# Attention steps of a cross-attention and expert kernel: a new order on three engines, and one 512 KB DMA that turns the two tiles of a head

## The reference

```python
q = jnp.einsum('bnd,de->bne', ln, Wq)                 # ln: normalised x
kv_in = jnp.concatenate([xn, ln], axis=1)             # 512 keys: context and x
kv = jnp.einsum('bnd,de->bne', kv_in, Wkv)
k, v = jnp.split(kv, 2, axis=-1)
q, k, v = (split_heads(q), split_heads(k), split_heads(v))
sim = jnp.einsum('bhid,bhjd->bhij', q * scale, k)
attn = jax.nn.softmax(jnp.where(full_mask[:, None, None, :], sim, max_neg), axis=-1)
out = jnp.einsum('bhij,bhjd->bhid', attn, v)
out = jnp.einsum('bne,ed->bnd', out.transpose(0, 2, 1, 3).reshape(b, m, INNER), Wout)
return layer_norm(out, g_o, b_o)
```

## Time and profile before

| | |
|---|---|
| median of 3 runs | 455.98 us (454.72 to 457.31) |
| the profiled execution | 455.38 us, its span 453.4 us |
| mean granted clock of TensorE, share of full | 0.945 |
| busy: PE, DVE, ACT, POOL | 371.8, 293.6, 263.7, 271.4 us |
| SP's DMA queue (q1), share of 16 engines over the span | 50.7% |
| transposes of tiles | 128, of 256 KB |

### The profile page before, as it was taken

How to read it: one execution, slowest core, us unless ns; L and a number is a source line. 1 busy time by engine, 2 the same in 40 slices (tenths; PEclk the granted TensorE clock), 3 DMA queues, 4 the chain that set the end, 5 groups by cost and what they waited for, 6 DMA issues and landing times. The chain is left out here.

```text
span 453.4 us, 7499 instructions
## 1 busy us (share of the span) xinstructions
PE 371.8 (82%) x2225; PEld 268.7 (59%) x2225; DVE 293.6 (65%) x732; ACT 263.7 (58%) x507; POOL 271.4 (60%) x346
## 2 busy tenths in 40 slices
PE   3669787887878888787889989886249999999996
PEld 2547565664656556465666657554137677777774
DVE  2888774747566574756556465660867777778885
ACT  3767866564645546464655646471058666666681
POOL 3231228677676767768676776872421677777681
PEclk9999998999999999999998989895559999999999
DMA  8200137967977979888999889799000000000001
GB/s 236 54 1 1 23 69 121 182 121 139 184 138 134 170 138 137 169 140 178 132 142 185 121 138 176 135 145 210 0 0 1 2 0 0 0 0 0 1 0 46
DMA packets 154913, 42.76 MB, mean 94 GB/s; under 512 B 144768, under 2 KB 154496, under 8 KB 154880
## 3 DMA queue, kind: packets, MB, share of 16 engines
q1 hardware_dynamic: 154448, 40.78, 50.7%
q10 hardware_dynamic: 432, 1.57, 1.1%
HBM read 8.26 MB, written 0.52 MB: 19 GB/s over the span
## 5 line engine op out<-in xcount | busy, mean ns | idle before, releaser
L394 POOL TENSOR_TENSOR p<-prob,p 128x512 f16<-128x512 f32 x128 | 147.4, 1163 | 90.5 <-ACT p L557 88.7
L549 ACT ACTIVATE prob<-sc,p_bias 128x512 f32<-128x512 f32 x128 | 91.0, 711 | 104.6 <-DVE p_bias L1155 104.5
L1146 DVE CUSTOM_DVE_ANT_0 sc<-ps,mask_add 128x512 f32<-128x512 f32 x128 | 83.0, 682 | 6.6 <-PE ps L706 4.9
L1180 DVE TENSOR_TENSOR q_lo<-ps,q_hi 128x512 fp32r<-128x512 f32 x32 | 22.1, 691 | 88.8 <-ACT q_hi L562 88.8
L704 PE MATMUL ps<-kv_hi,q_hi 128*128 128x512 f32 x128 | 53.5, 418 | 23.4 <-DVE neg_max L1146 23.4
L802 PE MATMUL ps<-pT,v 128*64 128x256 f16 x768 | 53.9, 296 | 4.4 <-DMA pT<-p 4.4
L1338 DVE TENSOR_TENSOR h<-h,ps 128x1024 f32<-128x1024 f32 (+1 forms) x32 | 39.1, 1221 | 18.9 <-PE ps L928 17.7
L802 PEld LDWEIGHTS ps<-pT,v 128*64 128x64 f16 x768 | 46.8, 120 | 6.2 <-issue 4.9
L706 PE MATMUL ps<-kv_hi,q_lo 128*128 128x512 f32 x128 | 50.2, 392 | 0.0
L705 PE MATMUL ps<-kv_lo,q_hi 128*128 128x512 f32 x128 | 50.1, 391 | 0.0
L704 PEld LDWEIGHTS ps<-kv_hi,q_hi 128*128 128x128 f32 x128 | 24.0, 187 | 40.0 <-DVE neg_max L1146 35.2
(11 more groups left out here) (193 smaller groups left out, 746.8 us busy)
## 6 DMA issues: line engine op xcount, KB each, us to landing
pT<-p SPq DMA_TRANSPOSE x128, 3.2
wup_s<-in_L_ffn_W_up SPq DMA_DIRECT2D x8, 256.0 KB, 3.4
wdn_s<-in_L_ffn_W_down SPq DMA_DIRECT2D x8, 256.0 KB, 3.7
wkv_s<-in_L_xattn_Wkv ACTq DMA_DIRECT2D x2, 512.0 KB, 7.1
x_in<-in_x SPq DMA_DIRECT2D x2, 256.0 KB, 8.1
wq_s<-in_L_xattn_Wq ACTq DMA_DIRECT2D x1, 512.0 KB, 7.6
tok<-in_ctx SPq DMA_DIRECT2D x4, 128.0 KB, 8.1
wo_s<-in_L_xattn_Wout SPq DMA_DIRECT2D x1, 512.0 KB, 5.4
```

What stands on the lines that cost most here:

```text
L394: pool.tensor_tensor(p16[:, t, 1, :], prob[:, t, :], p16[:, t, 0, :], ALU.subtract).then_inc(s_plo, 1)
L549: act.activation(prob[:, t, :], sc[:, t, :], ACT.Exp, bias=p_bias[:, t:t + 1], scale=-1.0, accum_out=p_sum[:, i % 2, t:t + 1]).then_inc(s_ ...
L1146: return dve.tensor_tensor_reduce(sc[:, t, :], ps[:, SCORE_BANK + (i * TILES + t) % SCORE_BANKS, :], mask_add[:, i % B, :], -SCALE, -LEAST ...
```

## The change

Four things change, all in the attention steps.

1. **One DMA for a head.** `turn_head` takes both tiles of a head in one transpose of 128 x 2048 values (512 KB). It waits for the low half of the head's second tile. `s_turned` has two semaphores, one for each head, and whoever waited for a tile's turn waits for the head's. `pT` is laid out with the tile outside the block of keys, so that the transpose writes one contiguous run of 16 blocks, and `attend` reads two runs of 128 queries per matmul.
2. **ACT**: exp 0, exp 1, high 0, high 1, query high half, exp 2, exp 3. The quarter of the queries is the one that PE computed in the step before.
3. **DVE**: the output of step i-3 is scaled at the head of the step; `shift_range(i, 2)` comes ahead of `invert(i - 1)`; the query's low half is that of the quarter that ACT now makes in this step.
4. **PE**: `project` behind `attend`. And `neg_max` and `p_bias` have a free element between two used ones.

```diff
@@ -83,7 +83,7 @@
             ("pick16", [P, E], F16), ("ones", [P, P], F32), ("range_v", [P, 8], F32),
-            ("neg_max", [P, TILES], F32), ("p_bias", [P, TILES], F32), ("p_sum", [P, 2, TILES], F32),
+            ("neg_max", [P, TILES, 2], F32), ("p_bias", [P, TILES, 2], F32), ("p_sum", [P, 2, TILES], F32),
             ("p_rinv", [P, 2, TILES], F32),
@@ -96,7 +96,7 @@
             ("p16", [P, TILES, 2, KEYS], F16),
-            ("pT", [P, 2, 2, 2 * KT, QT, P], F16), ("rinv_sb", [P, S], F32), ("ao", [P, S], F32),
+            ("pT", [P, 2, 2, QT, 2 * KT, P], F16), ("rinv_sb", [P, S], F32), ("ao", [P, S], F32),
         ])
@@ -226,7 +226,7 @@
         s_squares, s_range = sem("s_squares"), sem("s_range")
-        s_turned = [sem(f"s_turned{t}") for t in range(TILES)]
+        s_turned = [sem(f"s_turned{head}") for head in range(2)]
@@ -309,17 +309,18 @@
-            def turn_p(i, t):
-
-                sp.wait_ge(s_plo, i * TILES + t + 1)
-                if t == 0 and i >= 2:
+            def turn_head(i, head):
+
+                sp.wait_ge(s_plo, i * TILES + (head + 1) * QT)
+                if head == 0 and i >= 2:
                     sp.wait_ge(s_av, i - 1)
-                sp.dma_start_transpose(pT[:, i % 2, t // QT, :, t % QT, :],
-                                       p16[:, t, :, :].rearrange("p a k -> p (a k)")).then_inc(s_turned[t], 16)
+                sp.dma_start_transpose(pT[:, i % 2, head, :, :, :].rearrange("p q k c -> p (q k) c"),
+                                       p16[:, head * QT:(head + 1) * QT, :, :].rearrange("p t a k -> p (t a k)"))\
+                    .then_inc(s_turned[head], 16)
             for i in range(STEPS):
-                for t in range(TILES):
-                    turn_p(i, t)
+                for head in range(2):
+                    turn_head(i, head)
                 if i % B == 2:
@@ -382,7 +383,7 @@
                 if i:
-                    pool.wait_ge(s_turned[t], 16 * i)
+                    pool.wait_ge(s_turned[t // QT], 16 * i)
                 pool.tensor_copy(p16[:, t, 0, :], prob[:, t, :]).then_inc(s_phi_pool, 1)
@@ -546,14 +547,14 @@
                     act.wait_ge(s_rinv, i - 1)
-                act.activation(prob[:, t, :], sc[:, t, :], ACT.Exp, bias=p_bias[:, t:t + 1],
+                act.activation(prob[:, t, :], sc[:, t, :], ACT.Exp, bias=p_bias[:, t, 0:1],
                                scale=-1.0, accum_out=p_sum[:, i % 2, t:t + 1]).then_inc(s_exp, 1)
...
                 if i:
-                    act.wait_ge(s_turned[t], 16 * i)
+                    act.wait_ge(s_turned[t // QT], 16 * i)
                 act.activation(p16[:, t, 0, :], prob[:, t, :], ACT.Copy).then_inc(s_phi_act, 1)
@@ -596,11 +597,11 @@
                 split_high(i, 0)
+                split_high(i, 1)
+                if 2 <= i <= STEPS - B + 1:
+                    q_high(i + 2, (i - 2) % B)
                 exp(i, 2)
-                split_high(i, 1)
                 exp(i, 3)
-                if i <= STEPS - B:
-                    q_high(i + 3, (i - 1) % B)
@@ -791,17 +792,17 @@
                 pair, b = i // B, i % B
-                for t in range(TILES):
-                    pe.wait_ge(s_turned[t], 16 * (i + 1))
+                for head in range(2):
+                    pe.wait_ge(s_turned[head], 16 * (i + 1))
                 if i:
...
                         cut = slice(head * DH, (head + 1) * DH)
-                        mm = pe.matmul(ps[cut, AV_BANK, 0:S],
+                        mm = pe.matmul(ps[cut, AV_BANK, 0:S].rearrange("p (q c) -> p q c", q=QT),
                                        v16[:, b * KT + j, v, pair * P + head * DH:pair * P + (head + 1) * DH],
-                                       pT[:, i % 2, head, p * KT + j, :, :].rearrange("p q c -> p (q c)"),
+                                       pT[:, i % 2, head, :, p * KT + j, :],
                                        start=(n == 0), stop=(n == len(terms) - 1), skip_group_check=True)
@@ -853,11 +854,11 @@
                         score_step(i, t)
-                if i >= 3:
-                    project(i - 3)
                 if i >= 2:
...
                     attend(i - 2)
+                if i >= 3:
+                    project(i - 3)
                 if i <= STEPS - B:
@@ -1145,14 +1146,14 @@
                                                 mask_add[:, i % B, :], -SCALE, -LEAST, ALU.add, ALU.min,
-                                                neg_max[:, t:t + 1]).then_inc(s_masked, 1)
+                                                neg_max[:, t, 0:1]).then_inc(s_masked, 1)
...
                     dve.wait_ge(s_exp, (i - 1) * TILES + t + 2)
-                dve.tensor_scalar(p_bias[:, t:t + 2], neg_max[:, t:t + 2], LN_RANGE16, None, ALU.add)\
+                dve.tensor_scalar(p_bias[:, t:t + 2, 0], neg_max[:, t:t + 2, 0], LN_RANGE16, None, ALU.add)\
                    .then_inc(s_bias, 1)
@@ -1249,17 +1250,17 @@
             for i in range(1, STEPS):
+                if i >= 3:
+                    normalise_out(i - 3)
                 mask_scores(i, 0)
                 mask_scores(i, 1)
-                if i >= 3:
-                    normalise_out(i - 3)
                 shift_range(i, 0)
...
                 mask_scores(i, 3)
+                shift_range(i, 2)
                 invert(i - 1)
-                shift_range(i, 2)
-                if i <= STEPS - B:
-                    q_low(i + 3, (i - 1) % B)
+                if 2 <= i <= STEPS - B + 1:
+                    q_low(i + 2, (i - 2) % B)
             normalise_out(STEPS - 3)
...
             normalise_out(STEPS - 2)
```

## The result

The changed kernel takes **467.84 us** (median of 4 runs, 467.01 to 469.08) beside 456.47 for the kernel before (4 runs, 454.72 to 457.31): a ratio of 1.0272, 95% interval 1.0240 to 1.0303, so 11.4 us slower by the medians, 12.4 by the ratio, where 4.8 were forecast. The profiled execution has a span of 466.5 us, 13.1 more than before.

A forecast was written before the change was run, and what follows sets the result against it. A POOL and `p_bias` loop of 7.92 us was taken to bound the step; the 7.90 us landing loop eats the order's gain. 455.38 + 1.8 (end) + 3 (halts) = 460.2 us, range 439 to 470.

The forecast's parts named there:

- What bounds the kernel now: Attention steps: a loop of waits through POOL and `p_bias`, 7.92 us, with one through DVE and ACT close by, 7.4.
- The order: New order on ACT, DVE and PE: by itself brings the step to about 7.1 us, 22 us over 28 steps.
- the free element: Gap in `p_bias` on DVE: nothing taken in the sum; if `p_bias` meets POOL's high halves, up to 17 us lost.
- the fast rival: Long transpose lands within 3.72 us, loop 7.25: 439.7 us, up to 457 if `p_bias` meets POOL; chance 0.19.
- the rival by which the order gains nothing: Order doesn't gain even without the DMA, as the query's wait binds PE; time 460 us, no separate chance given.
- X: Time from issue to landing of a 512 KB transpose: 4.37 us, paced by how fast the issue hands out pieces.
- the second head's loop: Landing, POOL's four instructions, issue, landing: 3.53 + X = 7.90 us, against a step of 7.92, eating the order's gain.
- The end: Last two attention steps, short before, no longer shorten because a loop over a landing doesn't: last landing +1.8 us.
- Halts: Program fetches stopping transposes: up to 8 of 12 hit one, up to 1 us each; +3 us, between 0 and 8.
- PE has 1.4 us of slack: PE in the attention step: moving `project` behind `attend` costs nothing.
- The cover that goes: Tiles landed in time for their next use before; now the first waits for the second, both for one landing.
- The signs: Expected: transposes landing after 4.3 to 4.5 us, DMA waits nearly every step, shorter `p_bias` wait, steps of 7.9 us.

The follow-up runs named there:

- e5: The kernel before the change, with only `p_bias` made by a `tensor_reduce` instead of a `tensor_scalar`: 439.60 us.
- e1: The changed kernel with the four tile DMAs of before in place of the two head DMAs, `pT` layout kept: 454.83 us.
- e4: The changed kernel with four tile DMAs and `p_bias` made by a `tensor_reduce`: 442.10 us.
- e11: The changed kernel with the 16 loads of expert weights issued behind the last transpose, not within the steps: 472.47 us.
- e12: The changed kernel with the first head turned by one DMA and the second head's tiles by two: 467.93 us.
- e15: The changed kernel with four tile DMAs and the 16 weight loads issued behind the last transpose: 465.44 us.
- e3: The changed kernel, head DMAs kept, with `p_bias` made by a `tensor_reduce` over pairs of maximum and constant: 466.96 us.

## Why the prediction was wrong

The sign was right, the size was not: +11.4 us, against +4.8. Two steps of the working failed, the gain of the order and the price of the halts.

- **What bounds the kernel now**: right, and worth more than all of the change. The loop through POOL and `p_bias` is 7.92; with the wait alone taken away the loop of 7.4 shows, at 7.35 (e5). One reading was off and nothing hangs on it: the slices of the earlier trace rows are six to nine tenths in the attention, not eight to nine.
- **The order** ("by themselves these edits would bring the step to about 7.1", 22 us): wrong. Alone it gives 0.8 us (e1). The step that failed is the one on the free element, "I take nothing for it in the sum, because there POOL is waiting for a landing". POOL waits for a landing in few steps, `p_bias` meets its subtractions, and the gap between the elements changes nothing. The two rules of the Trainium skill that I set against this edit (SBUF — State Buffer, Who interferes with whom; Vector Engine (DVE) Microarchitecture Reference, Performance modes) agree with that: `p_bias` takes 0.69 us beside POOL's subtraction with the gap, 0.72 without. I used them only for the fast rival. The loop through ACT and PE, which I had at 7.0 to 7.2, shows without the lock at 7.30 (e4). So the rival by which the order gains nothing came true, though for this reason and not for PE's wait.
- **X and the second head's loop**: right in size, and with it the fast rival (3.72 or less) fell. The reason behind X was not: issues of 512 KB took 1.32 us at times and 2.73 at others, with the same landing after 4.26, so the issue doesn't pace the pieces, and that the sum came so near is partly luck. 4.25 against 4.37, so 7.79 in place of 7.90; side by side with the lock's loop the plain step is 7.82. This term came out at -2.6 us over 26 steps, not at zero.
- **The end**: right in kind. The last steps aren't short any more; from exponential 0 of step 29 to the last landing the change takes 2.1 more.
- **Halts** ("I take +3, between 0 and 8"): this term was mis-sized and decides. Against tile DMAs in the same order the steps cost 11.2 us more (e1), against the kernel before 8.5 + 2.6 = 11.1 over plain ones. I put the late tiles down to program fetches alone. That is part of it: in e11, where no loads are left in the steps, only transposes with a fetch in flight are late; and in e12, which loses as much as the change, all but one of the first head's late landings have a fetch in flight, and only two a load. The earlier trace rows counts 12 fetch packets; the same view has 12 more on another queue (q14). The other part I never priced: the 16 weight loads, which stand in SP's own list in every fourth step. Taking them out of the steps removes 8.2 of the 11.2, or 6.0 by the medians (e11, e15).
- **"PE has 1.4 us of slack"** holds while landings are in time (e1, clock 0.99). With head DMAs TensorE's clock fell to half in seven stretches of the 26 steps, and a landing 1.86 late came out as 2.63. I had priced a halt at no more than its own delay, and the clock at nothing.
- **The cover that goes**: I wrote that such delays were mostly covered before. The amount could have been estimated: a tile's loop is about a microsecond shorter than the step (some 6.7 us by the sum set down ahead of e4), the second head's 0.03 (7.79 and 7.82). A loop without slack has nothing to cover a delay with.
- **The signs**: "the waits name the DMA in nearly every step" and "ACT's wait for `p_bias` shrinks" both failed. They aren't bound to each other either: with the lock in place POOL waited for a landing 20 times in e11, about 1.1 us in each of its steps 8 to 20, in steps of the same 7.8 us. The two loops are so close that either can hold the step. ACT's wait for `p_bias` went down to 82.5 us with the reduction (e3), from 95.8 with the change.

## What to carry to other kernels

Before merging transfers in a loop, list what else the DMA engines carry meanwhile, loads in the same queue and fetches of the program alike, and compare the slack of the loop before and after: with a merged transfer whose loop is as long as the step each delay is lost time, while its undisturbed landing shows nothing. If a tiny instruction ends each time with another engine's long one, change its form first and reorder afterwards; here that gave 16 us where the order gave 1, and with that done one moved instruction gave 12 more.

## What the runs showed of the hardware

- A DVE `tensor_scalar` over two elements, with a free one between them, ends with POOL's running subtraction (0.69 us, the change); a `tensor_reduce` with the same output doesn't (0.16, e3).
- An undisturbed transpose of 512 KB lands 4.25 us after its issue, one of 256 KB 3.1 to 3.2. The landing does not follow the issue's length, as I had assumed for the pace of its pieces: with the change an issue of 1.32 us (step 1) and one of 2.73 (step 3) both land after 4.26.
- Two loads of 256 KB ahead of a 512 KB transpose in its queue delay its landing: 5.08 us on average over the seven of the steps, against 4.37 for the same seven without the loads (e11).
- In e11 a 512 KB transpose with no program fetch starting in its flight lands within 4.29 us (29 of 29); of the 25 with one, 14 take 4.5 to 5.9.
- TensorE's granted clock over the same steps was 0.94 with head DMAs, 0.99 with tile DMAs, and 0.99 with head DMAs and no loads among them, in one and the same order of PE.
- With matmuls in the loop that sets the step, a stretch at half clock makes it longer by itself: 1.07 us in step 15 of the change, 1.39 in e12 (10.49 against 9.10 us for nearly the same wait).
